# First chunk of a fused Mamba and FFN layer: the bias gating leaves VectorE for ScalarE and GpSimd, and the out-projection's weights are scaled one quad sooner

## The reference, cut to what matters

```python
mod = (_silu(L0_c) @ L0_wmod).reshape(2, 6, 1, -1)          # sa, ca, ga, sb, cb, gb
ga = sign(ga) * maximum(abs(ga), 0.25);  gb = the same of gb
h = layernorm(x) * (1 + ca) + sa
x = x + ga * mamba(h)          # in-proj, conv, scan over 2048 rows, gate, out-proj
h = layernorm(x) * (1 + cb) + sb
x = x + gb * (sum_r(h @ factors[r]) / sqrt(8) + bias)
```

## Time and profile before

| | |
|---|---|
| median of 3 runs | 2020.2 us (2019.19 to 2021.31) |
| profiled execution | 2021.83 us, of which the span from first to last instruction is 2020.1 us |
| PE busy | 1761.3 us (87%) |
| DVE busy | 1854.8 us (92%) |
| ACT busy | 1546.6 us (77%) |
| POOL busy | 1823.7 us (90%) |
| longest waits | ACT for DVE's products 308.8 us, PE's weight loads for POOL's products 169.4 us |

### The profile page before, as it was taken

The page is one execution under the profiler, slowest core; times in us unless marked ns, Lnnn a source line. Parts: engine busy times, 40 slices in busy tenths (PEclk is TensorE's granted clock), DMA queues, the critical chain, the costliest instruction groups (busy, mean ns, idle before and its releaser), DMA issues. The chain is left out here.

```text
span 2020.1 us, 29641 instructions
## 1 busy us (share of the span) xinstructions
PE 1761.3 (87%) x9128; PEld 1304.6 (65%) x9128; DVE 1854.8 (92%) x2219; ACT 1546.6 (77%) x4897; POOL 1823.7 (90%) x757
## 2 busy tenths in 40 slices
PE   7985988989889898988989898898988989898798
PEld 5664757657576665757667576766757576575664
DVE  2798999999999999999999999999999999999995
ACT  3766778687877878878787887878787787978763
POOL 1789999899999999999999999999989999999992
PEclk9896999999999999999999999999999999999898
DMA  5656514032140412304032240403213041321300
GB/s 171 235 115 153 141 48 157 22 111 89 36 154 15 149 48 86 114 22 157 22 140 71 109 141 22 157 22 131 69 70 122 31 142 36 105 69 37 111 27 32
DMA packets 72003, 186.19 MB, mean 92 GB/s; under 512 B 6818, under 2 KB 8482, under 8 KB 63908
## 3 DMA queue, kind: packets, MB, share of 16 engines
q1 hardware_dynamic: 68148, 176.95, 25.9%
q0 software_dynamic: 3696, 7.34, 2.2%
HBM read 172.20 MB, written 12.06 MB: 91 GB/s over the span
## 5 line engine op out<-in xcount | busy, mean ns | idle before, releaser
L597 POOL TENSOR_TENSOR ub<-u,b_all 128x2048 f32<-128x2048 f32 x255 | 1164.4, 4566 | 47.2 <-DMA b_all<-bc_scratch 47.2
L753 ACT ACTIVATE decay<-dt,decay_rate 128x256 f32<-128x256 f32 (+1 forms) x2048 | 888.3, 465 | 27.5 <-DVE state_p L1504 26.9
L1504 DVE TENSOR_TENSOR_SCAN decay<-decay,carry,ub 128x512 f32<-128x512 f32 x589 | 746.5, 1276 | 26.3 <-ACT decay L753 26.2
L615 POOL TENSOR_TENSOR state_p<-state_p,c_all 128x1024 f32<-128x1024 f32 (+1 forms) x256 | 525.7, 2054 | 108.4 <-ACT carry L737 83.6
L1504 DVE TENSOR_TENSOR_SCAN state_p<-decay,carry,ub 128x512 f32<-128x512 f32 x435 | 552.6, 1273 | 39.9 <-ACT decay L753 39.7
L1071 PE MATMUL y_bank<-ident,sc_d 128*128 128x128 f32 x2356 | 353.7, 282 | 95.9 <-DVE sc_d L1519 95.8
L1519 DVE TENSOR_TENSOR sc_d<-decay,c_all 128x512 f32<-128x512 f32 x589 | 394.8, 671 | 5.9 <-PE y_bank L1071 5.0
L1071 PEld LDWEIGHTS y_bank<-ident,sc_d 128*128 128x128 f32 x2356 | 279.5, 145 | 147.3 <-DVE sc_d L1519 137.5
L1071 PE MATMUL y_bank<-ident,state_p 128*128 128x128 f32 x1740 | 246.6, 283 | 123.8 <-POOL state_p L615 122.6
L1071 PEld LDWEIGHTS y_bank<-ident,state_p 128*128 128x128 f32 x1740 | 201.4, 144 | 223.8 <-POOL state_p L615 169.4
L737 ACT ACTIVATE carry<-decay 128x2 f32<-128x2 f32 x589 | 98.5, 167 | 312.3 <-DVE sc_d L1519 308.8
(11 more groups left out here) (141 smaller groups left out, 1831.9 us busy)
## 6 DMA issues: line engine op xcount, KB each, us to landing
win_h<-win_m SPq DMA_DIRECT2D x128, 256.0 KB, 2.6
win_z<-win_m SPq DMA_DIRECT2D x128, 256.0 KB, 2.9
b_all<-bc_scratch SPq DMA_DIRECT2D x31, 1024.0 KB, 4.7
c_all<-bc_scratch SPq DMA_DIRECT2D x31, 1024.0 KB, 5.4
xa<-x SPq DMA_DIRECT2D x16, 512.0 KB, 4.9
xc<-x SPq DMA_DIRECT2D x16, 512.0 KB, 3.8
out<-xc SPq DMA_DIRECT2D x15, 512.0 KB, 3.8
ffn<-factors POOLq DMA_DIRECT2D x7, 1024.0 KB, 10.2
```

Source lines behind the costliest of these rows:

```text
L597: pool.tensor_tensor(ub[:, slot, :, :, :], u[:, (PAIRS * c + q) % U_PAIRS, :, :].unsqueeze(1).to_broadcast([P, QUAD, 2, ROWS]), b_all[:, n ...
L615: pool.tensor_tensor(part, part, c_all[:, n:n + k, :].unsqueeze(2).to_broadcast([P, k, 2, ROWS]), ALU.mult).then_inc(pooled, 1)
L753: last = act.activation(bk[:, j * ROWS + j:(j + 1) * ROWS], dt[:, pair % DT_PAIRS, j, j:], ACT.Exp, scale=decay_rate[:, e, n:n + 1])
L1504: dve.tensor_tensor_scan(dst, bk[:, :], ub[:, quad % UB_RING, i, :, :].rearrange("p j r -> p (j r)"), carried_in[:, n, 2 * q:2 * q + 1], A ...
```

## The change

ScalarE multiplies the bias rows by sqrt(8) in step 14 of chunk 0 (`grow_bias`), POOL multiplies them with `bias_gate` at the end of quad 9 (`scale_bias`), and DVE's instruction in step 20 is gone. `keep_wo` moves from quads 6, 7, 9, 10 to 5, 6, 8, 9, and `scale_wo` from 7, 8, 9, 11 to 6, 7, 8, 10. Nothing is changed on PE or in SP's list.

```diff
+            def scale_bias():
+
+                pool.wait_ge(bias_grown, 1)
+                pool.wait_ge(bias_gated, 16 * BATCH)
+                pool.tensor_tensor(bias_row[:, :], bias_row[:, :], bias_gate, ALU.mult).then_inc(bias_scaled, 1)
...
-                    if c == 0 and g in (6, 7, 9, 10):
-                        keep_wo({6: 0, 7: 1, 9: 2, 10: 3}[g])
-                    if c == 0 and g in (7, 8, 9, 11):
-                        scale_wo({7: 0, 8: 1, 9: 2, 11: 3}[g])
+                    if c == 0 and g in (5, 6, 8, 9):
+                        keep_wo({5: 0, 6: 1, 8: 2, 9: 3}[g])
+                    if c == 0 and g in (6, 7, 8, 10):
+                        scale_wo({6: 0, 7: 1, 8: 2, 10: 3}[g])
+                    if c == 0 and g == 9:
+                        scale_bias()
...
+            def grow_bias():
+                act.wait_ge(bias_loaded, 16 * BATCH)
+                act.activation(bias_row[:, :], bias_row[:, :], ACT.Copy, scale=math.sqrt(RANK)).then_inc(bias_grown, 1)
...
+                    if c == 0 and s == 14:
+                        grow_bias()
...
-            def scale_bias():
-                dve.wait_ge(bias_loaded, 16 * BATCH)
-                dve.wait_ge(bias_gated, 16 * BATCH)
-                dve.scalar_tensor_tensor(out=bias_row[:, :], in0=bias_row[:, :], scalar=math.sqrt(RANK), in1=bias_gate,
-                                         op0=ALU.mult, op1=ALU.mult).then_inc(bias_scaled, 1)
...
-                    if c == 0 and s == 20:
-                        scale_bias()
```

More of the change, by code:

```diff
@@ L310, in build @@
         consts_made, rate_exp, cond_tanh, prep = sem("consts_made"), sem("rate_exp"), sem("cond_tanh"), sem("prep")
+        bias_grown = sem("bias_grown")
         bias_scaled, mods_copied, mods_turned = sem("bias_scaled"), sem("mods_copied"), sem("mods_turned")
```

## The result

The changed kernel takes 2028.07 us (median of 7 runs, 2025.5 to 2028.51) against 2020.2 (median of 7, 2019.19 to 2021.69): 7.9 us slower, ratio 1.0034 with a 95% interval of 1.0025 to 1.0044. The forecast was 2028.4. The changed kernel's seven times lie in two groups, three from 2025.5 to 2026.4 and four from 2028.1 to 2028.5, and the profiled execution is one of the first group.

What follows compares the result with a forecast made beforehand. POOL's list was taken to bound quads 7 to 11 of chunk 0, DVE's list after: keep_wo(1) at 133.7 plus 46.66 puts multiply_c(11) at 180.4, DVE 8.2 us later, so 2028.4 us against the median 2020.2; range 2021.5 to 2031.5.

Steps and rivals of the forecast that it cites:

- POOL's list up to multiply_c(11) is the chain: Chunk 0, quads 7 to 11: POOL's list bounds; the change is worth what it does to multiply_c(11)'s start.
- DVE's port wait lies in its shade: Chunk 0: removing DVE's bias instruction, up to 9.83 us, is worth 0 while POOL's chain is no shorter.
- keep_wo(1) would wait for a store that SP can't issue sooner: Chunk 0: store 0 goes out at 125.7 at the earliest, 0.95 us sooner; landing taken as 133.7.
- my two bounds of 133.2 and 134.2: Store 0's landing: 133.2 if it again takes 7.5 us from 125.7, 134.2 if it lands as before.
- POOL's sum of 46.66 us: POOL from keep_wo(1)'s start to multiply_c(11): 37.98 before, plus 9.24 of added work, less 0.56.
- The 0.56 us that I took for POOL's loss at the port: keep_wo(2) takes 2.88 us instead of 2.32; the 0.56 was counted as gained back on POOL.
- POOL's idle time: POOL stands still before keep_wo(1) from 124.05 to 133.7, 9.6 us, against 1.50 + 1.89 = 3.39 before.
- multiply_c(11) at 180.4, DVE's third product at 184.1, all later quads 8 us later: Quad 11 on POOL, then quad 12 on DVE: product 8.2 us later than 175.96, the shift lasting to the end.
- The bias product on POOL: End of quad 9: product of two partitions x 512, bounds 0.21 and 1.27 us, taken as 1.22.
- ScalarE's copy: Chunk 0: ACT gets one Copy of 512 elements, 0.59 us; cost 0, or 0.6 without cover by its waits.
- the store lands fast: Rival A: store 0 takes 2.6 us, keep_wo(1) starts at 128.3, multiply_c(11) at 175.0: +2.8, 2023.0 us; chance 0.11.
- keep_wo(1) hardly waits: Rival B: SP reaches its store much sooner, POOL goes on at 124.05, multiply_c(11) at 170.7: 2018.7 us; chance 0.08.

Runs made afterwards that it cites:

- the fastest version: Changed kernel with keep_wo(0) and scale_wo(0) in quad 4, other keep_wo in quads 5, 6, 8, stores 0 and 1 issued earlier, scale_wo(3) behind multiply_c(11): 2009.12, then 2010.29 us.
- e1: Bias part of the change alone, keep_wo and scale_wo left in the quads of the kernel before: 2019.76 us, ratio 0.9998.
- e3: Changed kernel with keep_wo(1) and keep_wo(2) writing into the two free halves of yg, SP's list in its old order: 2016.77 us, ratio 0.9983.
- e6: Changed kernel with the first store ahead of the win_h loads for chunk 2 in SP's list: 2018.83 us, ratio 0.9993.
- the idle time filled: Changed kernel with keep_wo(0) and scale_wo(0) in quad 4, the other quarters in quads 5 to 9, stores 0 and 1 issued earlier: 2014.69 us, ratio 0.9962.

## Why the prediction was right

- **That POOL's list up to multiply_c(11) is the chain, and DVE's port wait lies in its shade: right.** The bias part alone costs 0.3 us on the chain and nothing measurable on the median, and leaving the product out gains 0.9, of which 0.6 is the store. In every kernel of the table but the last DVE's third product follows multiply_c(11) by 3.3 to 3.8 us; in the last, where DVE's wait has come onto the chain, by 4.9.
- **That keep_wo(1) would wait for a store that SP can't issue sooner: right.** Forecast: issue at 125.7 and landing at 133.7. Measured, in the clock of before: issue at 125.74, and POOL goes on at 133.65. The latency was 7.8 us, not the 7.5 of before, and so between my two bounds of 133.2 and 134.2. The 134.2 that I had set beside it by the Trainium skill (DMA: Bandwidth & Descriptors, "HWDGE ordering") comes out half a microsecond too late, which is no test of that rule.
- **Why that store is slow: the factor's DMA, not the copies.** I had named both. The traces tell them apart. Over the eleven of them, 22 stores of this size were issued 2.5 to 4.7 us behind a factor's accumulating DMA, and all took 6.6 to 8.6 us and landed within 0.8 us of the landing of that DMA, also the fifteen that had no small copies just ahead of them, such as the fourth store of the kernel before (issued at 168.25, 6.7 us). The other 22 took 2.6 to 3.7 us. In the changed kernel the factor issued at 121.65 landed at 132.47 and the store at 131.99. By these rows its landing depended little on when SP got to it, as long as that was behind the factor's issue, and it fits that the landing came only 0.6 us sooner than before, though the store went out 0.9 us sooner. This is read from rows that stand side by side; no run took the factor away.
- **POOL's sum of 46.66 us: right to 0.2, with 0.2 of it a misread row.** It took 46.84 (132.07 to 178.91). The 0.56 us that I took for POOL's loss at the port were misread. The changed kernel has no such product on DVE, and its keep_wo(2) is followed after the same 2.89 us: it is POOL catching up after a DMA issue. The port's price is in the next instruction of the trace of before, scale_wo(2), 156.23 to 158.88 = 2.65 in place of 2.31 (153.60 to 155.91 with the product left out), so 0.34 where I had taken off 0.56.
- **POOL's idle time: 8.62 for 9.6.** The missing microsecond is the same lag: POOL was still at work when I had it waiting.
- **multiply_c(11) at 180.4, DVE's third product at 184.1, all later quads 8 us later:** 180.5 and 183.8. The distance between the two is 3.31 us here and not the 3.78 of before, because POOL was not running behind at that point (multiply_c(11) shows 1.25 us, before 1.71). DVE waited in a fourth place that I had not named, 2.26 us for ACT's decays before quad 11's first scan; it decided nothing. The shift stays in the profile through chunk 1, and 1.7 us of it go in chunk 2 as told above.
- **The median, 2028.07 for 2028.4: in part luck.** The chain supports the 8 us, but not a hit within 0.3. The half of the change that shifts the chain by the same 8.2 us moved its median by 6.2, and the changed kernel's own times lie in two groups some 2 us apart, of which the median falls into the later one.
- **The bias product on POOL, 1.22 of bounds 0.21 and 1.27: 1.22** (164.41 to 165.63, in the row above 1.26 long). ScalarE's copy took 0.61 us for the 0.59 of its price, and with the whole bias part costing 0.3 us no loss from it is seen.
- **Rivals.** That the store lands fast took an issue ahead of the factor's DMA: with the store ahead it landed in 2.8 us, in the changed kernel, beside the factor's DMA, in 7.8. That keep_wo(1) hardly waits was made true by two edits and gave 2018.83 and 2016.77, where I had put 2018.7.

## What to carry to other kernels

A stall of 9.9 us on the engine with the highest busy share is worth what the chain says and not what it lasts: here less than half a microsecond, and 5 to 6 us once the list of another engine was shortened. Before an instruction is moved up in its engine's list, ask what it waits for and whether that moves too; here the producer came 8.6 us sooner, but its store stood in a third engine's in-order list and went out behind another engine's large DMA, and the wait took two more instructions hostage. If a wait is the suspect, remove its reason in two unrelated ways (its place in the queue, another buffer): the same gain from both names the cause.

## What the runs showed of the hardware that was not expected

- **DVE's two-input instruction waited through several POOL instructions.** In the trace of before it came at 146.80 and got the port only at about 156.1 (an estimate: its end at 156.70 less the 0.6 us from start to start of DVE's products of 512 elements), after four POOL instructions had followed one another (starts at 147.67, 152.13, 153.35 between); with the bias back on DVE in the fastest version it took 9.00 us again. With the quarters alone moved it came at 157.13 and was through in 1.87, at the end of the one POOL instruction that was running. In the two slow cases POOL was running half a microsecond or more behind its starts (4.97 to 5.50 us shown for make_ub), in the quick one it was not (4.54). What decides it is not shown: these three cases of the instruction are all there is here, and no run was made to test it.
- **A factor's DMA issue mostly costs POOL about half a microsecond more than its row's distance shows.** Its successors start 0.82 us later as if nothing were, but show 0.5 us more each, 1.0 after two issues and 1.5 after three, until POOL next waits. A sum by distances between starts is short by that much wherever a wait doesn't absorb it. There are exceptions: the issue in quad 10 of the changed kernel (171.30, shown as 0.80 us in place of 1.24 to 1.29) leaves POOL no later, and the same holds in the three others that have the bias product in quad 9 and that issue in the same place (e1, e3 and e6); with the idle time filled it is 0.3. Why is open.
- **A 512 KB store issued 2.5 to 4.7 us behind a 1 MB accumulating DMA lands when that one lands**, 6.6 to 8.6 us after its issue, in 22 of 22 cases; otherwise it takes 2.6 to 3.7 us, also when it is issued near the end of such a DMA (115.97 behind one of 106.36: 2.84 us). The copies of 2 KB take 4.6 to 6.3 us beside that DMA, and 2.1 to 2.5 us where they are issued 1 to 2 us ahead of it.
